# One-hot matrices of eight blocks by one comparison, and counting that waits for its own constants only

## The chip, the cores and the metric

The kernel runs on one core of one Trainium2 chip. The time is the device time of one execution in microseconds (us); of several runs the median is given. The core has five engines with instruction streams of their own that meet only through semaphores: TensorE (PE, with its weight loads as PEld), VectorE (DVE), ScalarE (ACT), GpSimd (POOL) and SyncE (SP), which here issues transfers. TensorE's granted clock is shown as a share of full speed (1.00 is 2.4 GHz, 0.50 is 1.2 GHz).

## The reference, cut to what matters

Two layers, each an attention and a mixture of experts, with a residual and a layer norm after each of the four. There are 2 x 2048 tokens of 128 numbers, so 4,096 tokens, 32 blocks of 128.

```python
x = layernorm(x + deltanet(x))
# experts, layer 0: one of 8 for each token
p = softmax(x @ gate_w); e = argmax(p); w = p[e]
x = layernorm(x + w * (gelu(x @ w1[e] + b1[e]) @ w2[e] + b2[e]))
x = layernorm(x + linear_attention(x))
# experts, layer 1: the best two of 8, weighted by a softmax over the two
logits = x @ Wr + br; (l, e) = top_k(logits, 2); c = softmax(l)
x = layernorm(x + sum(c[i] * (silu(x @ W1[e[i]]) * (x @ W3[e[i]])) @ W2[e[i]] for i in (0, 1)))
```

## The kernel before

The kernel sorts the tokens by expert before it multiplies. In the middle stage (`single_experts`, followed by `linear_attention` in the same block) a group is one of 8 experts, and the sorted tokens fill up to 39 tiles of 128 rows. In the pair stage (`stage_pairs`) a group is one of 28 pairs of experts, padded to half tiles, and there are up to 46 tiles. Before a stage can multiply it needs the sorted order. This is the routing, and it is the same in both stages:

- SP stores all tokens to a scratch tensor in memory, `xe_dram` (L1044 in the middle, L1852 in the pair stage), in one transfer. In the middle, ten other transfers stand ahead of it in SP's queue: the biases and what `linear_attention` will need.
- VectorE picks each token's group and writes `sel`, a 0/1 matrix in fp16 (L1219, L2096).
- TensorE counts (L1109, L1931): one small matmul for each group, which gives the tokens of each group in each block.
- VectorE multiplies the counts by a triangle (`upto`, L1225, L2101), TensorE adds them up over the blocks, and VectorE works out for every token its slot in the sorted order, and from it `col`, the tile, and `pos`, the row in the tile.
- The order has to be inverted: for each tile and row, which token stands there. For each of the 32 blocks VectorE makes a one-hot matrix `at_pos` (128 tokens x 128 rows; L1241, L2118) and a matrix `at_col` (128 tokens x 39 or 46 tiles) that holds the token's number, `code`, at its tile (L1242, L2119). TensorE multiplies the two and sums over the blocks (L1118, L1944). It waits before each block's matmul for the semaphore `hot`, which each `at_col` raises.
- VectorE reads the result into `read_at` (L1244; in the pair stage L2124 and L2125) and raises `decoded`. GpSimd waits for `decoded` and for `stored`, the landing of `xe_dram`, and then gathers the tiles' rows, one tile after another (L1094, L1909).
- VectorE works out which expert or pair each tile belongs to. TensorE packs these numbers into words with the matrix `pack` (L1122, L1948), VectorE copies them (L1249, L2137) and raises `read`. SP waits for `stored` and then `read` before it issues the weights of the tiles (L1051, L1861).

GpSimd fills the constants at the start of each stage. The semaphore `const` counts them. In the middle, 1 stands for the plain fills, 2 for the triangles `before` and `tri`, and 10 for the eight steps that fill `pack` (L1088). In the pair stage, 3 stands for everything but `pack`, and 7 for `pack` too. TensorE waits for the last of them ahead of counting (10 or 7); so does VectorE (10 ahead of `upto` in the middle, 7 ahead of `sel` in the pair stage).

In the middle, TensorE's stream has another piece of work between placing and the one-hot matmuls: `ready(pe)`, the preparation of the attention's weights (L1471, L1475, L1477, L1480), which waits for GpSimd and ScalarE.

The helper `link` raises a semaphore with an instruction and makes VectorE wait for it, because the next one reads its result. `spread(ap, n)` repeats each element of a row n times, innermost; `every(ap, n)` repeats the whole row n times.

Of the kernel before, what the change touches and what calls it, by code (L numbers as in the profile page):

```python
# [9 lines left out]
ALU = mybir.AluOpType  # L10
# [3 lines left out]
P = 128  # L14
B, L, D = 2, 2048, 128
BLOCKS = B * L // P
# [15 lines left out]
def spread(ap, n):  # L32

    return ap.unsqueeze(len(ap.shape)).broadcast_to([*ap.shape, n])
# [913 lines left out]
F16 = mybir.dt.float16  # L948
# [3 lines left out]
GR = (B * L + PAIRS * (HALF - 1)) // P + 1  # L952
ROUND = float(3 * 2 ** 22)
# [15 lines left out]
TILES = (B * L + E * (P - 1)) // P  # L969


def single_experts(nc, io, sb, tag, st, banks, w_in, wa, wb, b2):
# [3 lines left out]
    PACK = 8  # L976
# [20 lines left out]
    slot, col, pos = (tmp(n, [P, BLOCKS]) for n in ("slot", "col", "pos"))  # L997
    col_no, pos_no, code = tmp("col_no", [P, TILES]), tmp("pos_no", [P, P], F16), tmp("code", [P, BLOCKS])
    at_pos, at_col = tmp("at_pos", [P, BLOCKS, P], F16), tmp("at_col", [P, BLOCKS, TILES], F16)
# [18 lines left out]
    b1_in, b1_ps, b1_done, y_done, ranked = (sem(n) for n in ("b1_in", "b1_ps", "b1_done", "y_done", "ranked"))  # L1018
# [84 lines left out]
    def tensor(pe, ready):  # L1103
        pe.wait_ge(b1_in, 16)
        nc.tensor.transpose(psY[0][:, 0:E * NF], b1_rows[:, :], ident[0:E * NF, 0:E * NF]).then_inc(b1_ps, 1)
        pe.wait_ge(const, 2 + PACK)
# [9 lines left out]
        for n in range(BLOCKS):  # L1116
            pe.wait_ge(hot, n + 1)
            mm = nc.tensor.matmul(ps_found, at_pos[:, n], at_col[:, n], start=(n == 0), stop=(n == BLOCKS - 1))  # L1118
        mm.then_inc(found, 1)
        pe.wait_ge(numbered, 1)  # L1120
        pe.wait_ge(decoded, 1)
# [80 lines left out]
    def vector(dve):  # L1202
        v = nc.vector
        links = 0

        def link(ins):

            nonlocal links
            links += 1
            ins.then_inc(step, 1)  # L1210
            dve.wait_ge(step, links)
# [11 lines left out]
        dve.wait_ge(const, 2 + PACK)  # L1223
# [14 lines left out]
        link(v.tensor_scalar(col[:, :], col[:, :], ROUND, -ROUND, ALU.add, ALU.add))  # L1238
        link(v.scalar_tensor_tensor(pos[:, :], col[:, :], -float(P), slot[:, :], ALU.mult, ALU.add))
        for n in range(BLOCKS):  # L1240
            v.tensor_scalar(at_pos[:, n], pos_no[:, :], pos[:, n:n + 1], None, ALU.is_equal)  # L1241
            v.tensor_scalar(at_col[:, n], col_no[:, :], col[:, n:n + 1], code[:, n:n + 1], ALU.is_equal, ALU.mult).then_inc(hot, 1)  # L1242
# [524 lines left out]
def stage_pairs(nc, io, sb, tag, v_in, wac, wb):  # L1767
# [7 lines left out]
    with ExitStack() as st:  # L1775
        def tmp(name, shp, dt=F32):
            return st.enter_context(nc.sbuf_tensor(f"{tag}_{name}", shp, dt))

        def sem(name):
            return take(nc, f"{tag}_{name}")  # L1780

        def bank(name, shp):
# [17 lines left out]
        slot, col, pos = (tmp(n, [P, BLOCKS]) for n in ("slot", "col", "pos"))  # L1800
        col_no, pos_no, code = tmp("col_no", [P, GR]), tmp("pos_no", [P, P], F16), tmp("code", [P, BLOCKS])
        at_pos, at_col = tmp("at_pos", [P, BLOCKS, P], F16), tmp("at_col", [P, BLOCKS, GR], F16)
# [21 lines left out]
        ranked = sem("ranked")  # L1824
# [7 lines left out]
        def every(ap, n):  # L1832

            return ap.unsqueeze(1).broadcast_to([ap.shape[0], n, ap.shape[1]])
# [12 lines left out]
        with nc.Block(no_gpsimd_drain=True) as block:  # L1847
# [79 lines left out]
            def _(pe):  # L1927
                pe.wait_ge(const, 7)
# [13 lines left out]
                for n in range(BLOCKS):  # L1942
                    pe.wait_ge(hot, n + 1)
                    mm = nc.tensor.matmul(ps_found, at_pos[:, n], at_col[:, n], start=(n == 0), stop=(n == BLOCKS - 1))  # L1944
                mm.then_inc(found, 1)
                pe.wait_ge(paired, 1)
                pe.wait_ge(decoded, 2)
# [115 lines left out]
            def _(dve):  # L2063
                v = nc.vector
                links = 0

                def link(ins):

                    nonlocal links
                    links += 1  # L2070
                    ins.then_inc(step, 1)
                    dve.wait_ge(step, links)
# [22 lines left out]
                dve.wait_ge(const, 7)  # L2095
# [19 lines left out]
                link(v.tensor_scalar(col[:, :], col[:, :], ROUND, -ROUND, ALU.add, ALU.add))  # L2115
                link(v.scalar_tensor_tensor(pos[:, :], col[:, :], -float(P), slot[:, :], ALU.mult, ALU.add))
                for n in range(BLOCKS):
                    v.tensor_scalar(at_pos[:, n], pos_no[:, :], pos[:, n:n + 1], None, ALU.is_equal)  # L2118
                    v.tensor_scalar(at_col[:, n], col_no[:, :], col[:, n:n + 1], code[:, n:n + 1], ALU.is_equal, ALU.mult).then_inc(hot, 1)  # L2119
# [128 lines left out]
```

## Time and profile before

| | us |
|---|---|
| median of 3 runs | 779.83 |
| the three runs | 779.83, 772.30, 779.96 |
| profiled execution | 777.14 |
| its span in the trace | 775.4 |
| middle stage: first constant to first gather | 285.6 to 307.7 |
| pair stage: first constant to first gather | 551.0 to 583.1 |

Within the span TensorE is busy 618.8 us (80%), its weight loads 466.9 us (60%), VectorE 425.0 us (55%), ScalarE 351.9 us (45%) and GpSimd 286.6 us (37%). These shares are means over stages that have different limits. In the two routings the first tile's matmuls have not begun, and each engine waits for the one before it, so there the order of the steps counts and not the share. A row of the timeline gives the start, the length, the engine, the line and the operation, what it writes and reads with shapes, and in brackets how long the engine sat idle before and what released it. The tensors of both stages have the prefix `e_`, those of the attention `a_`; the memory banks of the middle stage are all called `mid_ps`.

### The profile page before, as it was taken

The page shows a single profiled execution, that of the slowest core. Times are in us where ns is not written, and L with a number is a line of the kernel's source. Part 1 is how long each engine was busy: PE and PEld are TensorE (multiplying, and loading weights), DVE is VectorE, ACT ScalarE, POOL GpSimd, SP SyncE. Part 2 cuts the span into 40 slices and gives each one's busy share as a digit, 9 for nine tenths or more (in the row PEclk, how much of TensorE's full clock was granted, in tenths as well). Part 3 has the DMA queues.
Part 4 walks back from the last instruction along what each step waited for, and adds up shares of the span by engine and source line. Part 5 has one row for each costly group of instructions (what it writes and reads, how often), then busy time and mean ns, then how long its engine had stood idle before and what let it go on. Part 6 is the DMA issues. An engine that isn't in the chain of part 4 may idle for free. (4 is left out here: it accounts for less than half of the span.)

```text
span 775.4 us, 40316 instructions
## 1 busy us (share of the span) xinstructions
PE 618.8 (80%) x16699; PEld 466.9 (60%) x16699; DVE 425.0 (55%) x1490; ACT 351.9 (45%) x935; POOL 286.6 (37%) x489
## 2 busy tenths in 40 slices
PE   4787545999998935899939899998147999999993
PEld 3665445988888923899926667666122455554552
DVE  4996370133332568155543546657594667767765
ACT  4764110222222660578843454644104555665562
POOL 2244302122211453444325336353404255455434
PEclk9997555799999685799976999999556999999997
DMA  4011112222222916566521111100063333333430
GB/s 122 2 39 39 38 54 71 71 91 92 92 85 76 339 53 123 173 194 210 171 62 46 36 28 37 30 27 8 1 110 82 94 102 110 100 100 106 104 96 12
DMA packets 70850, 66.45 MB, mean 86 GB/s; under 512 B 17183, under 2 KB 60366, under 8 KB 70512
## 3 DMA queue, kind: packets, MB, share of 16 engines
q1 hardware_dynamic: 65488, 55.43, 23.5%
q0 software_dynamic: 5280, 10.00, 6.1%
q8 instruction: 42, 0.69, 0.4%
q14 instruction: 40, 0.33, 0.2%
HBM read 20.70 MB, written 11.93 MB: 42 GB/s over the span
## 5 line engine op out<-in xcount | busy, mean ns | idle before, releaser
L1962 PE MATMUL e_psH<-wac,e_xT 128*64 x184 | 91.4, 620 | 0.8 <-ACT e_xT L2022 0.6
L1964 PE MATMUL e_psH<-e_up_w,e_xT 128*64 128x512 f32 x184 | 91.4, 621 | 0.0
L1909 POOL DMA_INDIRECT e_row<-xe_dram,e_read_at x46 | 44.6, 970 | 73.7 <-DVE spare L2150 45.3
L1914 POOL DMA_INDIRECT out<-spare,e_write_at x46 | 46.3, 1007 | 47.3 <-ACT spare L2039 36.9
L596 POOL TENSOR_TENSOR tb<-tinv,mb 128x128 f32<-128x128 f32 x64 | 24.3, 401 | 85.4 <-PE d_psY L610 85.4
L1094 POOL DMA_INDIRECT e_row<-xe_dram,e_read_at x39 | 37.0, 948 | 49.4 <-DVE spare L1258 34.6
L2143 DVE TENSOR_TENSOR e_h<-e_pre,e_psH 128x512 f32<-128x512 f32 x46 | 31.6, 687 | 42.9 <-ACT e_pre L2028 42.9
L2028 ACT ACTIVATE e_pre<-e_psH 128x512 f32<-128x512 f32 x46 | 27.5, 598 | 58.4 <-PE e_psH L1964 57.9
L1983 PE MATMUL e_psY<-vb,e_hT 128*64 x368 | 50.8, 282 | 2.9 <-issue 2.9
L1180 ACT ACTIVATE e_hT<-mid_ps,e_b 128x128 f32<-128x128 f32 x156 | 45.0, 381 | 15.1 <-PE mid_ps L1136 14.9
L1986 PE MATMUL e_psY<-e_down_w,e_hT 128*64 128x128 f32 x368 | 50.8, 282 | 0.0
L721 DVE TENSOR_TENSOR S<-d_psS,on 128x64 f32<-128x64 f32 x64 | 14.3, 223 | 60.7 <-PE d_psS L667 60.7
L1983 PEld LDWEIGHTS e_psY<-vb,e_hT 128*64 128x64 f32 x368 | 39.6, 138 | 10.7 <-issue 10.7
L1136 PE MATMUL mid_ps<-e_xT,e_up_w 128*128 128x128 f32 x312 | 44.4, 289 | 0.2 <-DMA e_up_w<-wa 0.2
L2016 ACT ACTIVATE e_up_w<-wac 128x512 f32 x46 | 28.8, 626 | 33.4 <-DVE e_words L2137 26.9
L1962 PEld LDWEIGHTS e_psH<-wac,e_xT 128*64 128x64 f32 x184 | 22.0, 139 | 34.4 <-issue 29.9
L1144 PE MATMUL mid_ps<-wb,e_hT 128*128 x312 | 42.2, 280 | 0.5 <-issue 0.4
L1973 PEld LDWEIGHTS e_psT<-ident,e_h 128*128 128x128 f32 x184 | 19.3, 140 | 36.7 <-issue 36.5
L1662 DVE TENSOR_TENSOR a_sc<-mid_ps,a_tri 128x512 f32<-128x512 f32 x64 | 40.9, 680 | 0.0
L1136 PEld LDWEIGHTS mid_ps<-e_xT,e_up_w 128*128 128x128 f32 x312 | 40.4, 202 | 0.6 <-issue 0.4
L1986 PEld LDWEIGHTS e_psY<-e_down_w,e_hT 128*64 128x64 f32 x368 | 39.6, 138 | 0.0
L1144 PEld LDWEIGHTS mid_ps<-wb,e_hT 128*128 128x128 f32 x312 | 38.7, 196 | 1.2 <-issue 1.0
(386 smaller groups left out, 1778.7 us busy)
## 6 DMA issues: line engine op xcount, KB each, us to landing
e_down_w<-vb SPq DMA_DIRECT2D x92, 128.0 KB, 2.0
e_up_w<-wa SPq DMA_DIRECT2D x39, 256.0 KB
xe_dram<-xe SPq DMA_DIRECT2D x2, 2080.0 KB, 13.2
vk_now<-vk SPq DMA_DIRECT2D x18, 192.0 KB, 2.1
kq_now<-kq SPq DMA_DIRECT2D x18, 192.0 KB, 2.1
gk_now<-gk SPq DMA_DIRECT2D x18, 128.0 KB, 2.0
outs_dram<-spare SPq DMA_DIRECT2D x9, 256.0 KB, 2.8
r<-in_L_attn_hidden_states SPq DMA_DIRECT2D x8, 256.0 KB, 4.6
```

The lines of the kernel that those rows point to most:

```text
L1094: pool.indirect_dma_start(out=row[g % ROWS][:, :], out_offset=None, in_=x_dram, in_offset=bass.IndirectOffsetOnAxis(ap=read_at[:, g:g + 1] ...
L1136: mm = nc.tensor.matmul(psH[g % 2][:, f], up_w[g % DEEP][:, f * P:(f + 1) * P], xT[g % 2][:, :], start=True, stop=True)
L1144: mm = nc.tensor.matmul(psY[g % 2][:, 0:D], hT[g % DEEP][:, f], wb[:, bass.ds(who * NF + f, 1)].rearrange("p a d -> p (a d)"), start=(f == ...
L1180: act.activation(hT[g % DEEP][:, f], psH[g % 2][:, f], ACT.Gelu, bias=b1[:, bass.ds(who * NF + f, 1)]).then_inc(h_done, 1)
L1662: ins = v.tensor_tensor(sc[:, g].rearrange("p k h l -> p (k h) l"), psS[g][:, :].rearrange("p (a l) -> p a l", l=HALF_T), tri[:, :].unsque ...
L1909: pool.indirect_dma_start(out=row[g % ROWS][:, :], out_offset=None, in_=x_dram, in_offset=bass.IndirectOffsetOnAxis(ap=read_at[:, g:g + 1] ...
L1914: pool.indirect_dma_start(out=out, out_offset=bass.IndirectOffsetOnAxis(ap=write_at[:, g:g + 1], axis=0), in_=z[:, g], in_offset=None, bou ...
L1962: nc.tensor.matmul(psH[g % 2][0:HALF, j], xT[g % 2][:, 0:HALF], wac[:, bass.ds(who[0][j], 1)].rearrange("p a f -> p (a f)"), start=True, s ...
L1964: mm = nc.tensor.matmul(psH[g % 2][HALF:P, j], xT[g % 2][:, HALF:P], up_w[g % 2][j][:, :], start=True, stop=True)
L1983: nc.tensor.matmul(psY[0:HALF, j], hT[g % 2][:, j, k * P:k * P + HALF], wb[:, bass.ds(who[0][j] * NF + k, 1)].rearrange("p a d -> p (a d)" ...
L1986: mm = nc.tensor.matmul(psY[HALF:P, j], hT[g % 2][:, j, k * P + HALF:(k + 1) * P], down_w[g % DEEP][:, j, k], start=(k == 0), stop=(k == N ...
L2143: v.tensor_tensor(h[g % 2][:, :, :], pre[g % 2][:, :, :], psH[g % 2][:, :, F:2 * F], ALU.mult).then_inc(h_done, 1)
```

## The change

For eight blocks at a time (`AHEAD = 8`), one `tensor_tensor` compares the numbers of the columns with `at`, one compares the numbers of the rows with `pos`, and one multiplies the first result by `code`. That is three instructions for eight blocks instead of two for each block. The small operands (`col_no`, `code`, and the new `at` and `pos`) become fp16, as `pos_no` and the results already are. `hot` is raised once in eight blocks, and TensorE waits for it before every eighth matmul. A new semaphore, `matched`, keeps the multiplication behind the comparison that it reads. The waits for `const` ahead of counting ask only for the constants that counting uses (2 and 3); the wait for `pack` stands before the matmul that reads it. The core of the diff, for the middle stage; the pair stage has the same with `GR` for `TILES`, 7 for `2 + PACK` and 3 for 2:

```diff
-    slot, col, pos = (tmp(n, [P, BLOCKS]) for n in ("slot", "col", "pos"))
-    col_no, pos_no, code = tmp("col_no", [P, TILES]), tmp("pos_no", [P, P], F16), tmp("code", [P, BLOCKS])
+    slot, col = tmp("slot", [P, BLOCKS]), tmp("col", [P, BLOCKS])
+    at, pos = tmp("at", [P, BLOCKS], F16), tmp("pos", [P, BLOCKS], F16)
+    col_no, pos_no, code = tmp("col_no", [P, TILES], F16), tmp("pos_no", [P, P], F16), tmp("code", [P, BLOCKS], F16)
...
-        pe.wait_ge(const, 2 + PACK)
+        pe.wait_ge(const, 2)
         pe.wait_ge(selected, 1)
...
         for n in range(BLOCKS):
-            pe.wait_ge(hot, n + 1)
+            if n % AHEAD == 0:
+                pe.wait_ge(hot, n // AHEAD + 1)
             mm = nc.tensor.matmul(ps_found, at_pos[:, n], at_col[:, n], start=(n == 0), stop=(n == BLOCKS - 1))
         mm.then_inc(found, 1)
         pe.wait_ge(numbered, 1)
+        pe.wait_ge(const, 2 + PACK)
...
-        dve.wait_ge(const, 2 + PACK)
+        dve.wait_ge(const, 2)
         dve.wait_ge(counted, 1)
...
-        link(v.tensor_scalar(col[:, :], col[:, :], ROUND, -ROUND, ALU.add, ALU.add))
-        link(v.scalar_tensor_tensor(pos[:, :], col[:, :], -float(P), slot[:, :], ALU.mult, ALU.add))
-        for n in range(BLOCKS):
-            v.tensor_scalar(at_pos[:, n], pos_no[:, :], pos[:, n:n + 1], None, ALU.is_equal)
-            v.tensor_scalar(at_col[:, n], col_no[:, :], col[:, n:n + 1], code[:, n:n + 1], ALU.is_equal, ALU.mult).then_inc(hot, 1)
+        link(v.tensor_scalar(at[:, :], col[:, :], ROUND, -ROUND, ALU.add, ALU.add))
+        link(v.scalar_tensor_tensor(pos[:, :], at[:, :], -float(P), slot[:, :], ALU.mult, ALU.add))
+        for c in range(BLOCKS // AHEAD):
+            s = slice(c * AHEAD, (c + 1) * AHEAD)
+            v.tensor_tensor(at_col[:, s], every(col_no[:, :], AHEAD), spread(at[:, s], TILES), ALU.is_equal).then_inc(matched, 1)
+            v.tensor_tensor(at_pos[:, s], every(pos_no[:, :], AHEAD), spread(pos[:, s], P), ALU.is_equal)
+            dve.wait_ge(matched, c + 1)
+            v.tensor_tensor(at_col[:, s], at_col[:, s], spread(code[:, s], TILES), ALU.mult).then_inc(hot, 1)
```

## Rows read from the trace of the kernel before

**Rows 1.** The page's part 4: the chain that ended last, by line.
```profile
PE e_psH L1962 11%; PE e_psY L1983 6%; PE e_psT L1973 3%; PE e_psX L1954 2%; DVE e_at_col L2119 1%; DVE e_at_pos L2118 1%; PE e_psY L1986 0%; DMA e_row<-xe_dram,e_read_at 0%; DMA e_br<-in_L_ffn_br 0%; POOL out L1914 0%; PE e_psX L1931 0%; PE e_psH L1964 0%; DVE e_picked L2110 0%; DVE e_upto L2101 0%; DVE e_sel L2096 0%
```

**Rows 2.** Timeline of the middle routing, 287 to 292: start, length, engine, line.
```profile
287.64 2.76 POOL L1088 TENSOR_SCALAR_AFFINE_SELECT e_pack<-e_pack 128x5 bf16<-128x5 bf16 x8
...
287.91 0.43 DVE L1219 TENSOR_TENSOR e_sel<-e_rank,e_key 128x256 f16<-128x256 f32 x1
...
288.70 0.35 DVE L1222 RECIPROCAL xe<-e_den 128x32 f32<-128x32 f32 x1
...
290.46 0.64 PE L1109 MATMUL mid_ps<-e_ones,e_sel 128*32 128x1 f16 x8 [3.01 <-POOL e_pack L1088]
...
290.74 0.38 SPq L1044 DMA_DIRECT2D xe_dram<-xe  x1
...
291.22 0.42 DVE L1225 TENSOR_TENSOR e_upto<-mid_ps,e_tri 32x264 f16<-32x264 f32 x1 [2.16 <-PE mid_ps L1109]
```

**Rows 3.** Timeline of the middle, from the one-hot loop to the first tile.
```profile
294.89 0.26 DVE L1241 TENSOR_SCALAR e_at_pos<-e_pos_no,e_pos 128x128 f16<-128x128 f16 x1
...
295.88 0.57 PE L1480 MATMUL mid_ps<-a_w,a_bo_mat 128*128 128x9 f32 x2 [0.36 <-ACT a_wY L1646]
...
296.30 0.45 PE L1118 MATMUL mid_ps<-e_at_col,e_at_pos 128*128 128x39 f16 x4
...
306.58 0.31 DVE L1242 TENSOR_SCALAR e_at_col<-e_col_no,e_col,e_code 128x39 f16<-128x39 f32 x1
...
306.94 0.22 PE L1118 MATMUL mid_ps<-e_at_col,e_at_pos 128*128 128x39 f16 x1 [0.15 <-DVE e_at_col L1242]
...
307.70 1.20 POOL L1094 DMA_INDIRECT e_row<-xe_dram,e_read_at  x1 [12.38 <-DVE e_read_at L1244]
...
308.18 0.15 DVE L1249 CAST e_words<-mid_ps 1x5 int32<-1x5 f32 x1 [0.26 <-PE mid_ps L1122]
...
309.47 15.45 SPq L1051 DMA_DIRECT2D e_up_w<-wa  x9
...
312.62 2.04 PE L1136 MATMUL mid_ps<-e_xT,e_up_w 128*128 128x128 f32 x8 [0.18 <-DMA e_up_w<-wa]
```

**Rows 4.** Transfers: the two writes, KB, us to landing; middle, then pair stage.
```profile
xe_dram<-xe SPq DMA_DIRECT2D x1, 2080.0 KB, 13.9
...
xe_dram<-xe SPq DMA_DIRECT2D x1, 2080.0 KB, 12.6
```

**Rows 5.** Timeline of the pair stage's routing, 553 to 584.
```profile
553.89 1.53 POOL L1893 TENSOR_SCALAR_AFFINE_SELECT e_pack<-e_pack 128x23 bf16<-128x23 bf16 x4 [0.16 <-POOL e_tri_no L1890]
...
559.89 1.09 DVE L2096 TENSOR_TENSOR e_sel<-e_pair_no,e_pair 128x896 f16<-128x896 f32 x1
...
560.90 0.25 DVE L2098 TENSOR_SCALAR e_den<-e_ex 128x32 f32<-128x32 f32 x1
...
562.13 0.36 SPq L1852 DMA_DIRECT2D xe_dram<-xe  x1
...
569.47 0.26 DVE L2118 TENSOR_SCALAR e_at_pos<-e_pos_no,e_pos 128x128 f16<-128x128 f16 x1
...
581.68 0.22 PE L1944 MATMUL e_psR<-e_at_col,e_at_pos 128*128 128x46 f16 x1 [0.15 <-DVE e_at_col L2119]
...
582.63 0.20 DVE L2125 TENSOR_TENSOR e_write_at<-e_token,e_empty 128x46 uint32<-128x46 f32 x1
...
583.12 1.07 POOL L1909 DMA_INDIRECT e_row<-xe_dram,e_read_at  x1 [21.02 <-DVE e_write_at L2125]
```

**Rows 6.** VectorE groups by form: busy us, mean ns of one, idle before.
```profile
L2118 DVE TENSOR_SCALAR e_at_pos<-e_pos_no,e_pos 128x128 f16<-128x128 f16 x32 | 8.1, 253 | 0.0
...
L2126 DVE TENSOR_SCALAR e_past<-e_ends,e_tile_no 128x28 f32<-128x28 f32 x1 | 0.2, 234 | 0.0
```

**Rows 7.** Windows: length, busy us (count) of PE, PEld, DVE, ACT, POOL, clock, DMA, GB/s.
```profile
312.00:321.00 9.00, 7.81 (x34) 7.28 (x35) 0.00 (x0) 5.03 (x16) 4.44 (x5) 0.50 0.60 193
321.00:324.00 3.00, 3.00 (x29) 3.00 (x28) 1.11 (x5) 1.76 (x7) 0.47 (x1) 0.99 0.32 122
588.00:594.00 6.00, 5.78 (x13) 1.50 (x15) 0.99 (x2) 2.61 (x4) 3.85 (x5) 0.50 0.74 202
```

More of the change, by code:

```diff
@@ L969 @@
 TILES = (B * L + E * (P - 1)) // P
+AHEAD = 8
 def single_experts(nc, io, sb, tag, st, banks, w_in, wa, wb, b2):
@@ L1017, in single_experts @@
         "read", "stored"))
-    b1_in, b1_ps, b1_done, y_done, ranked = (sem(n) for n in ("b1_in", "b1_ps", "b1_done", "y_done", "ranked"))
+    b1_in, b1_ps, b1_done, y_done, ranked, matched = (sem(n) for n in ("b1_in", "b1_ps", "b1_done", "y_done", "ranked", "matched"))
     row_in = [sem(f"row_in{i}") for i in range(ROWS)]
@@ L1799, in stage_pairs @@
         halves, ends, first, one = (tmp(n, [P, PAIRS]) for n in ("halves", "ends", "first", "one"))
-        slot, col, pos = (tmp(n, [P, BLOCKS]) for n in ("slot", "col", "pos"))
-        col_no, pos_no, code = tmp("col_no", [P, GR]), tmp("pos_no", [P, P], F16), tmp("code", [P, BLOCKS])
+        slot, col = tmp("slot", [P, BLOCKS]), tmp("col", [P, BLOCKS])
+        at, pos = tmp("at", [P, BLOCKS], F16), tmp("pos", [P, BLOCKS], F16)
+        col_no, pos_no, code = tmp("col_no", [P, GR], F16), tmp("pos_no", [P, P], F16), tmp("code", [P, BLOCKS], F16)
         at_pos, at_col = tmp("at_pos", [P, BLOCKS, P], F16), tmp("at_col", [P, BLOCKS, GR], F16)
@@ L1823, in stage_pairs @@
             "hot", "found", "decoded", "paired", "packed", "read", "stored", "bias_in"))
-        ranked = sem("ranked")
+        ranked, matched = sem("ranked"), sem("matched")
         row_in = [sem(f"row_in{i}") for i in range(ROWS)]
@@ L1927, in _ @@
             def _(pe):
-                pe.wait_ge(const, 7)
+                pe.wait_ge(const, 3)
                 pe.wait_ge(selected, 1)
@@ L1942, in _ @@
                 for n in range(BLOCKS):
-                    pe.wait_ge(hot, n + 1)
+                    if n % AHEAD == 0:
+                        pe.wait_ge(hot, n // AHEAD + 1)
                     mm = nc.tensor.matmul(ps_found, at_pos[:, n], at_col[:, n], start=(n == 0), stop=(n == BLOCKS - 1))
@@ L1946, in _ @@
                 pe.wait_ge(paired, 1)
+                pe.wait_ge(const, 7)
                 pe.wait_ge(decoded, 2)
@@ L2094, in _ @@
                 link(v.scalar_tensor_tensor(pair[:, :], hi[:, :], 0.5, lo[:, :], ALU.mult, ALU.subtract))
-                dve.wait_ge(const, 7)
+                dve.wait_ge(const, 3)
                 v.tensor_tensor(sel[:, :, :], every(pair_no[:, :], BLOCKS), spread(pair[:, :], PAIRS), ALU.is_equal).then_inc(selected, 1)
@@ L2114, in _ @@
                 link(v.tensor_scalar(col[:, :], slot[:, :], 1.0 / P, -127 / 256, ALU.mult, ALU.add))
[L2115 to L2119, printed above, removed]
+                link(v.tensor_scalar(at[:, :], col[:, :], ROUND, -ROUND, ALU.add, ALU.add))
+                link(v.scalar_tensor_tensor(pos[:, :], at[:, :], -float(P), slot[:, :], ALU.mult, ALU.add))
+                for c in range(BLOCKS // AHEAD):
+                    s = slice(c * AHEAD, (c + 1) * AHEAD)
+                    v.tensor_tensor(at_col[:, s], every(col_no[:, :], AHEAD), spread(at[:, s], GR), ALU.is_equal).then_inc(matched, 1)
+                    v.tensor_tensor(at_pos[:, s], every(pos_no[:, :], AHEAD), spread(pos[:, s], P), ALU.is_equal)
+                    dve.wait_ge(matched, c + 1)
+                    v.tensor_tensor(at_col[:, s], at_col[:, s], spread(code[:, s], GR), ALU.mult).then_inc(hot, 1)
                 dve.wait_ge(found, 1)
```

## Prediction

> **What bounds the kernel now.** I read the page first, then the chain of waits, then the timelines of the two routings, then single rows for durations. The chain that ended last [rows 1] shows the reader two things. The tail of the kernel is TensorE work of the pair stage (L1962, L1983, L1973), and in front of it stands the routing of that stage, with the two operations of the one-hot loop, `e_at_col` L2119 and `e_at_pos` L2118, as the largest VectorE entries. So what the routing of the pair stage saves arrives at the end one for one: nothing of the stage can start before the first gather. The chain ends at the start of that stage, so for the middle stage the waits have to be read in the program and the timeline.
>
> In the middle stage the order is: selection, counting, placing, 32 pairs of comparisons, decode, gather. Counting does not start when `e_sel` is ready (288.34) but when GpSimd's last fill of `e_pack` is (287.64 + 2.76 = 290.40), and TensorE starts at 290.46 [rows 2]. The one-hot loop then runs on VectorE from 294.89 to 306.89, its last matmul starts at 306.94, and the first gather at 307.70 [rows 3]. But the gather has a second condition, `stored`: the 2,080 KB write of `xe_dram` was issued at 290.74 [rows 2] and landed 13.9 us after its issue [rows 4], at 304.64. At present it is 3.06 us early. That is the cover I must not forget.
>
> In the pair stage `e_pack` was filled at 553.89 + 1.53 = 555.42, and `e_sel`, which comes before counting, only began at 559.89. The loop runs from 569.47, the last matmul starts at 581.68, the first gather at 583.12 [rows 5]. The write of `xe_dram`, issued at 562.13 [rows 5], landed after 12.6 us [rows 4], at 574.73, 8.4 us ahead of the gather.
>
> **The waits on constants.** In the pair stage all the waits for 7 were met 4.5 us before they were reached [rows 5], so 7 to 3 gives nothing. In the middle, counting may start at 288.34 plus the hand-over from `e_sel` to TensorE; the second constant is filled before `e_pack` (from 287.64) and is there. Where the last `at_col` released its matmul (306.89 to 306.94) the hand-over took 0.05 us [rows 3]; I take 0.1. That is 288.44 instead of 290.46, so 2.0 us. `e_upto` stood 0.76 us behind the start of counting (290.46 to 291.22) [rows 2]; it moves with it to 289.2. Its engine is free by then: the reciprocal ahead of it ended at 289.05 [rows 2]. The wait for all of `const` now stands before the matmul for the packed words, where it has long been met (290.40). What TensorE has queued between placing and the one-hot matmuls is the preparation for the attention stage; its last piece, L1480 at 295.88, hangs on GpSimd and ScalarE, not on counting, and does not move [rows 3]. It has a cost only if the first eight blocks are ready before it: they come at about 294.8, so the first group waits until 296.4, which the later groups absorb.
>
> **The one-hot loop.** Per block it issued one comparison for `at_pos` and one compare-and-multiply for `at_col`. 32 pairs took 12.0 us in the middle (294.89 to 306.89), 0.375 us a pair [rows 3]. It now issues three `tensor_tensor` per eight blocks: 8x39 or 8x46 elements, 8x128, and 8x39 or 8x46 again. The duration is the unknown. From the two rows of `e_sel`, 256 elements take 0.43 us and 896 take 1.09 us [rows 2, 5]: 0.66 us for 640 elements is 1.03 ns an element, and I take 1.04. From start to start, `e_sel` with 896 elements held the engine for 1.01 us (559.89 to 560.90) [rows 5], so an instruction costs 75 ns beyond its elements (0.935). Both are with a 32-bit source; the change has 16-bit sources only.
>
> Pair stage: 8x46 is 368 elements, 0.46 us; 1,024 elements, 1.14 us; 0.46 us again. That is 2.06 us a group, 8.25 us for four, plus 0.07 us for the drain of the last instruction and 0.06 us to TensorE. The wait on `matched` costs nothing, since the long `at_pos` comparison lies between the two instructions on `at_col`. The price of groups is at the end: before, one matmul was left after the last comparison; now eight are. Where four stood ready together, they took 0.45 us [rows 3], of which one is about 0.22 us, so a further matmul costs 0.08 to 0.11 us; seven at 0.10 are 0.7 us. The last matmul starts 8.25 + 0.13 + 0.7 = 9.08 us after the loop's start, where it was 12.21 us (569.47 to 581.68) [rows 5]. **Gain 3.1 us.** TensorE needs 0.8 us for a group and VectorE 2.06 us, so TensorE does not become the bound. The write, landed at 574.73, stays ahead of a gather at about 580.0.
>
> Middle: 312 elements cost 0.40 us, so 1.95 us a group and 7.8 us for four. First start to last matmul is 7.8 + 0.13 + 0.7 = 8.6 us against 12.05 (294.89 to 306.94) [rows 3], 3.4 us less. With the 2.0 us of the waits, the gather's addresses would be ready for 307.70 - 5.4 = 302.3. There the write is in the way: 304.64 at the earliest, 304.9 with the 0.29 us from the end of `e_write_at` (582.83) to the first gather as it stands in the pair stage [rows 5]. **Gain 2.8 us, not 5.4**; 2.6 us are lost on the write. The write itself is not moved: the ten transfers ahead of it in SP's queue hold it, not the routing. The expert weights of the first tile follow `stored` too: SP issued them at 309.47, 1.1 us after the words were stored (308.33) [rows 3]; the words now come before the landing, so it is 304.7 plus 1.1, 305.8, and they stay just ahead of the second transpose. So L1136, at 312.62 before, comes at 309.8.
>
> `pos` and `at` as 16-bit outputs have 32 elements each; their nearest rows are equally short and I put no cost on them, between 0 and 0.05 us. The bound of the element rate is open on both sides. Below: a one-source operation with 16-bit data, 128 elements, takes 253 ns, where one with 28 32-bit elements and the same pointer takes 234 ns [rows 6], 0.2 ns an element; so narrow data can be faster on this engine. Above: no row shows two 16-bit sources of which one repeats an element. I take 1.04 ns, the rate of the nearest row, `e_sel`, which has two sources with both kinds of repetition.
>
> The Trainium skill, page "Vector Engine (DVE) Microarchitecture Reference", section "Performance modes", lets a two-source operation produce two results a cycle when all operands are 16-bit and the innermost step of each is one; it reports that one element read 16 times as a source of such an operation ran at one result a cycle. Here one source of each of the three instructions repeats its element innermost, so by this page the narrow types buy no rate and the sum stays at 5.9 us; were the mode taken it would be 9.6 us, rival (a). No row here shows either.
>
> **The sum.** 2.8 + 3.1 = 5.9 us. The profiled execution took 777.14 us (775.4 us of span and 1.74 us around it), so 771.2 us. The median of the three runs shown is 779.83, which gives 773.9; the runs reach from 772.3 to 779.96, and the profiled one is between. I name 773.0.
>
> **Rivals.** (a) *Two elements a cycle.* Half the elements: 1.14 us a group in the pair stage, 5.4 us in all, gain 6.8; the write (574.73) is then still ahead of the gather (576.3). The middle stays at 2.8. Together 9.6 us: 767.5 for the profiled execution. For it: the one-source 16-bit row; against it: the repeated element. (b) *The write does not bind.* Then the middle gives 5.4 and the sum is 8.5: 768.6. For it: the same write took 1.3 us less in the pair stage [rows 4], so its length is not fixed; against it: nothing in the change makes it 2.3 us shorter. (c) *TensorE's clock takes it back.* After both routings TensorE works at half its clock (0.50, that is 1.2 GHz) until 321 and 594 [rows 7], some 8 us after its work begins in the middle (312.62) [rows 3] and 6 us in the pair stage. If these rises stay at their time instead of following the work, half of each stage's gain is lost: 1.4 and 1.55 us, sum 2.9, 774.2. (d) *Slower.* If the repeated 16-bit reads run below one element a cycle, the pair stage breaks even at (12.21 - 0.83 - 0.9) / 7.04 = 1.49 ns an element. In the middle the loop may take 14.05 us, and the limit is (14.05 - 1.73) / 6.59 = 1.87 ns. Both together turn at 1.67 ns. At two cycles an element (2.09 ns) the pair stage loses 4.2 and the middle 1.5 us: 782.8, slower than before. Against it: `e_sel` repeats too and holds 1.04.
>
> **How the numbers follow.** Forecast 0.72, (a) 0.08, (b) 0.04, (c) 0.12, (d) 0.04. About 1% (7.8 us) is what a measurement of this kernel can tell from no change. (a) and (b) are faster by over 1%; the forecast's 5.9 us lies below the bound, but the runs scatter by 7.7 us, and I give a fifth of it to the far side: faster 0.26. Slower by over 1% needs 2.2 ns an element or a disturbed comparison: 0.03. The rest, 0.71, is within 1%. The range: below, the fastest run less the sum, 772.3 - 5.9 = 766.4, which holds (a) and (b) for the profiled execution; above, 779, near the median less nothing, which holds (c) on the median (776.9) and leaves out (d).
>
> **What would show it.** In the profile after: `e_upto` of the middle about 2 us earlier; 1,024-element comparisons of 1.2 us (0.6 would be (a), 2.2 would be (d)); loops of 7.8 and 8.25 us; last matmul 0.7 us behind the last multiplication; the first gather of the middle right behind the landing at 304.6 with `e_read_at` over 2 us earlier ((b) if it comes at 302.3); the first gather of the pair stage 5.9 us earlier than 583.12. The prediction is wrong if the clock rises late in both stages, or if the write's landing moves.

## The result, and the profile after

| | before | after |
|---|---|---|
| median of 20 runs each, us | 779.68 | 771.33 |
| lowest run, us | 772.30 | 766.28 |
| profiled execution, us | 777.14 | 769.71 |
| its span, us | 775.4 | 768.0 |
| granted TensorE clock, mean | 0.854 | 0.871 |

The ratio of the runs is 0.9934, with a 95% interval from 0.9912 to 0.9957: about 5.1 us less (0.0066 x 779.68). The forecast was 773.0 and within 1%. The medians stand further apart (8.35 us, a quotient of 0.9893, which lies outside that interval), and the profiled executions 7.4 us. I go by the ratio, because it has an interval and because ten further runs of the changed kernel (e5 below) came out at 0.9938 again, there with medians 5.9 us apart. One run of each kernel was far off the others: 999.18 us before, and 806.44 us after, at a granted clock of 0.758.

First the timeline of the middle stage of the changed kernel (start and length in us, engine, line, operation, and in brackets the engine's idle time ahead and what ended it):

```profile
283.75 0.35 SPq L1042 DMA_DIRECT2D e_b_rows<-in_L_ffn_b  x1
...
287.42 0.42 DVE L1229 TENSOR_TENSOR e_upto<-mid_ps,e_tri 32x264 f16<-32x264 f32 x1 [0.15 <-PE mid_ps L1111]
...
288.94 0.38 SPq L1046 DMA_DIRECT2D xe_dram<-xe  x1
...
291.04 0.48 DVE L1246 TENSOR_TENSOR e_at_col<-e_col_no,e_at 128x312 f16<-128x312 f16 x1
291.11 1.79 POOL L1410 TENSOR_SCALAR a_tri_b<-a_tri_b,a_low 128x64 f32<-128x64 f32 x1
...
295.85 0.60 PE L1487 MATMUL mid_ps<-a_w,a_bo_mat 128*128 128x9 f32 x2 [0.85 <-POOL a_bo_mat L1418]
...
299.25 0.45 PE L1121 MATMUL mid_ps<-e_at_col,e_at_pos 128*128 128x39 f16 x8 [1.47 <-DVE e_at_col L1249]
299.73 0.20 DVE L1251 TENSOR_SCALAR e_read_at<-mid_ps 128x39 uint32<-128x39 f32 x1 [0.54 <-PE mid_ps L1121]
...
304.00 1.20 POOL L1096 DMA_INDIRECT e_row<-xe_dram,e_read_at  x1 [6.64 <-DMA xe_dram<-xe]
```

SP's transfer in the first row waits for nothing of the routing, so I measure every kernel's middle stage from it: it is at 283.75 here, 285.54 before. From there `e_upto` comes at 3.67 us (before 5.68), the last group of one-hot matmuls at 15.50 (before the last matmul at 21.40), `e_read_at` at 15.98, and the first gather at 20.25 (before 22.16). The last row names the new bound: GpSimd sat idle until the *write* of `xe_dram`, where before it sat idle until `e_read_at` [rows 3]. The addresses were ready at 299.93 and lay for four microseconds.

The same for the pair stage:

```profile
548.82 0.35 SPq L1858 DMA_DIRECT2D e_br<-in_L_ffn_br  x1
...
567.26 0.54 DVE L2129 TENSOR_TENSOR e_at_col<-e_col_no,e_at 128x368 f16<-128x368 f16 x1
567.72 1.22 DVE L2130 TENSOR_TENSOR e_at_pos<-e_pos_no,e_pos 128x1024 f16<-128x1024 f16 x1
568.86 0.53 DVE L2132 TENSOR_TENSOR e_at_col<-e_at_col,e_code 128x368 f16<-128x368 f16 x1
569.31 0.53 DVE L2129 TENSOR_TENSOR e_at_col<-e_col_no,e_at 128x368 f16<-128x368 f16 x1
...
575.57 0.49 PE L1953 MATMUL e_psR<-e_at_col,e_at_pos 128*128 128x46 f16 x8 [1.55 <-DVE e_at_col L2132]
...
577.27 1.06 POOL L1917 DMA_INDIRECT e_row<-xe_dram,e_read_at  x1 [17.39 <-DVE e_write_at L2138]
```

A group takes 2.05 us (567.26 to 569.31). From SP's first transfer of the stage the loop starts at 18.44 us (before 18.48), and the first gather comes at 28.45 (before 32.13). Here it is `e_write_at` that ends the wait, as before [rows 5]; the write has long landed.

### The profile page after: what moved, and what is told of

It reads as the page before. It is cut to its first block and busy times, and to the rows that moved or that the text cites. A ratio compares the mean times of both kernels' runs of the same rounds, so it can differ in the third digit from the quotient of the medians.

```text
span 768.0 us, 40212 instructions
## 1 busy us (share of the span) xinstructions
PE 601.2 (78%) x16699; PEld 457.2 (60%) x16699; DVE 416.7 (54%) x1386; ACT 351.7 (46%) x935; POOL 290.3 (38%) x489
## 5 line engine op out<-in xcount | busy, mean ns | idle before, releaser
L1184 ACT ACTIVATE e_hT<-mid_ps,e_b 128x128 f32<-128x128 f32 x156 | 45.0, 381 | 14.0 <-PE mid_ps L1140 13.9
```

The lines of the kernel that those rows point to most:

```text
L1184: act.activation(hT[g % DEEP][:, f], psH[g % 2][:, f], ACT.Gelu, bias=b1[:, bass.ds(who * NF + f, 1)]).then_inc(h_done, 1)
```

## Experiments

The experiments ran in three groups, each beside its own runs of the kernel before: the first four kernels (before: 776.09 us), the next three (775.36), and the last two on another chip, on which the kernel before itself took 821.41 us; times are compared inside a group, by their ratio. Distances are counted as above, from SP's first transfer of the stage, and this table holds them (us). The column on the pair stage's matmuls gives the start of the last group of eight, or of the last single one in the two kernels with the old loops:

| kernel | middle: `e_read_at` | write issued | it took | first gather | first up matmul | pair stage: last matmuls | first gather | ratio to before (95%) |
|---|---|---|---|---|---|---|---|---|
| before | 21.66 | 5.20 | 13.9 | 22.16 | 27.08 | 30.69 | 32.13 | 1 |
| after | 15.98 | 5.19 | 14.2 | 20.25 | 25.35 | 26.75 | 28.45 | 0.9934 (0.9912 to 0.9957) |
| e1_waits_only | 19.85 | 5.20 | 14.1 | 20.36 | 25.35 | 30.65 | 32.08 | 0.9942 (0.9910 to 0.9974) |
| e2_onehot_only | 17.69 | 5.20 | 14.7 | 20.79 | 25.91 | 26.75 | 28.45 | 0.9973 (0.9932 to 1.0014) |
| e3_wide_operands | 15.99 | 5.20 | 13.5 | 19.63 | 24.82 | 26.79 | 28.50 | 0.9918 (0.9889 to 0.9948) |
| e4_pairs_packed | 15.99 | 5.19 | 14.1 | 20.19 | 25.26 | 23.08 | 25.21 | 0.9857 (0.9794 to 0.9920) |
| e5_changed_again | 15.99 | 5.20 | 14.5 | 20.56 | 25.63 | 26.74 | 28.45 | 0.9938 (0.9899 to 0.9977) |
| e6_early_write | 21.92 | 3.21 | 16.6 | 22.43 | 27.36 | 26.75 | 28.45 | 0.9961 (0.9915 to 1.0007) |
| e7_packed_early | 20.98 | 3.21 | 15.5 | 21.49 | 26.43 | 23.11 | 25.25 | 0.9914 (0.9879 to 0.9950) |
| e8_packed_again | 15.99 | 5.20 | 13.8 | 19.93 | 25.07 | 23.09 | 25.23 | 0.9867 (0.9833 to 0.9902) |
| e9_late_loads | 17.28 | 3.20 | 13.9 | 18.01 | 23.54 | 23.81 | 25.94 | 0.9866 (0.9831 to 0.9902) |

**One half of the change at a time.** The first kernel has the new waits on constants and the old loops; the second the new loops and the old waits:

```
e1:  - pe.wait_ge(const, 2 + PACK)     + pe.wait_ge(const, 2)      # and as changed elsewhere
     the loops of 32 blocks as before
e2:  - pe.wait_ge(const, 2)            + pe.wait_ge(const, 2 + PACK)
     the loops of four groups as changed
```

> The kernel before with the waits for constants of the change and its old one-hot loop. Times are counted from SP's first transfer of the stage (285.54 before, 283.75 in the changed kernel). Theory W (the landing of the write of xe_dram bounds the middle once the routing is faster): counting starts 2.0 us earlier, the addresses are ready at about 19.9 instead of 21.9, just behind the landing (5.2 + 13.9 to 14.2 = 19.1 to 19.4), and the first gather moves from 22.2 to 20.2, nearly where the changed kernel has it (20.25). The pair stage keeps its 32.1 us from the first transfer to the first gather. In all 2.0 us less, 0.26%. Rival A (the two edits add up in the middle): the gather moves by the 2.0 us here as well, but then the loop alone must show as much again. Rival N: the wait for the packing constants was covered by something else, and the gather stays at 22.2.

> The changed kernel with the old waits for constants. Theory W: counting starts 2.0 us later than in the changed kernel, the loop takes as long, the addresses are ready at about 18.0 to 18.4, still ahead of the write's landing at 19.1 to 19.4, so the first gather of the middle stays at 20.25 and the kernel costs the same as the changed one: the waits are worth nothing beside the loop. Rival A: the first gather comes 2.0 us later than in the changed kernel, at 22.2 less the gain of the loop. In the pair stage the last one-hot matmul stands 8.6 us behind the loop's start in both theories, against 12.2 before.

The waits alone bring the middle's gather to 20.36, 1.80 us earlier; with the one-hot groups added it is 20.25. So in the middle stage the two halves don't add up (1.80 and 1.37 us alone, 1.91 together): each alone brings the routing to the write, and the later gather of e2 (20.79) goes with a write that took 0.5 us longer. In the pair stage it is the other way round: the waits give nothing (32.08 against 32.13) and the groups everything (28.45, as in the whole change). The middle of e1, near the gather:

```profile
301.53 0.20 DVE L1245 TENSOR_SCALAR e_read_at<-mid_ps 128x39 uint32<-128x39 f32 x1 [0.31 <-PE mid_ps L1118]
302.04 1.20 POOL L1094 DMA_INDIRECT e_row<-xe_dram,e_read_at  x1 [10.58 <-DVE e_read_at L1245]
```

and of e2:

```profile
299.63 0.20 DVE L1250 TENSOR_SCALAR e_read_at<-mid_ps 128x39 uint32<-128x39 f32 x1 [0.54 <-PE mid_ps L1121]
302.73 1.20 POOL L1096 DMA_INDIRECT e_row<-xe_dram,e_read_at  x1 [9.71 <-DMA xe_dram<-xe]
```

In e1 the gather stands 0.31 us behind the end of the addresses; the write had landed at 300.98 (281.68 + 5.20 + 14.1), 1.06 us before it; with the 0.86 to 0.93 us that a gather needs behind a landing, it could have gone at most 0.2 us earlier. In e2 the addresses had been ready for 2.9 us, and the gather stands 0.89 us behind the landing (281.94 + 5.20 + 14.7 = 301.84). The times of the whole kernel can't tell the halves apart: their intervals overlap, and the gains at stake are 1.9 to 5.6 us, against runs that scatter by over 10. They even stand in the wrong order: by the gathers e1 gains 1.85 us and e2 5.05, by the ratios it is 0.58% (4.5 us) and 0.27% (2.1 us). Over all ten kernels the check is better. The gains of the two gathers, each from one profiled execution and taken as a share of the kernel before, run from 0.24% in e1 to 1.26% in e9. They lie inside the interval of the ratio for nine of the ten, and for e1 just below it (0.26% to 0.90%).

**The width of the operands.** Everything as in the changed kernel, but `at`, `pos`, `code` and the column numbers in 32 bits. The row numbers `pos_no` and the one-hot matrices stay at 16:

```
- at, pos = tmp("at", [P, BLOCKS], F16), tmp("pos", [P, BLOCKS], F16)
+ at, pos = tmp("at", [P, BLOCKS]), tmp("pos", [P, BLOCKS])
- col_no, ..., code = tmp("col_no", [P, GR], F16), ..., tmp("code", [P, BLOCKS], F16)
+ col_no, ..., code = tmp("col_no", [P, GR]), ..., tmp("code", [P, BLOCKS])
```

> The changed kernel with at, pos, code and the column numbers in 32 bits; the row numbers and the two results stay 16-bit. Theory R (one of the two sources repeats an element, and so the narrow types buy no rate): the comparison of 1,024 elements takes 1.22 us as in the changed kernel, the loop of the pair stage 8.6 us, the time is the same within 0.3%. Rival: the 16-bit sources do help, and the comparison takes clearly over 1.22 us here. Open beside it: in the changed kernel GpSimd's small operations next to the middle loop took up to 1.79 us where they took 0.45 before. If that comes from long two-source VectorE operations it stays; if from 16-bit sources it goes.

The 1,024-element comparison by tile, in e3 (count; min/median/max ns; first and last start; form), where one source is 32-bit:

```profile
L2130 DVE TENSOR_TENSOR e_at_pos<-e_pos_no,e_pos x4: 1215/1216/1218, 570.8 to 576.9; 128x1024 f16<-128x1024 f16 x4
```

and in the changed kernel, where both are 16-bit:

```profile
L1247 DVE TENSOR_TENSOR e_at_pos<-e_pos_no,e_pos x4: 1210/1260/1354, 291.4 to 297.6; 128x1024 f16<-128x1024 f16 x4
...
L2130 DVE TENSOR_TENSOR e_at_pos<-e_pos_no,e_pos x4: 1217/1218/1219, 567.7 to 573.8; 128x1024 f16<-128x1024 f16 x4
```

1,216 and 1,218 ns: the narrow types buy nothing here. (A row gives the type of one source only; that `pos` is 32-bit in e3 is in its code.) All that was won in the loop is the number of instructions.

**The same elements in another order.** Is it the repeated element? In the pair stage the number of the block was made the innermost index, so that the source with one value for each block is read with step one, and the source with the numbers is stored eight times over (the middle stage is left as it was):

```
+ col_no = tmp("col_no", [P, GR, AHEAD], F16); pos_no = tmp("pos_no", [P, P, AHEAD], F16)
+ at_pos = tmp("at_pos", [P, BLOCKS // AHEAD, P, AHEAD], F16)      # at_col likewise
- v.tensor_tensor(at_pos[:, s], every(pos_no[:, :], AHEAD), spread(pos[:, s], P), ALU.is_equal)
+ v.tensor_tensor(at_pos[:, c], pos_no[:, :, :], every(pos[:, s], P), ALU.is_equal)
- mm = nc.tensor.matmul(ps_found, at_pos[:, n], at_col[:, n], ...)
+ mm = nc.tensor.matmul(ps_found, at_pos[:, n // AHEAD, :, n % AHEAD], at_col[:, n // AHEAD, :, n % AHEAD], ...)
```

> The changed kernel; in the pair stage alone the eight blocks lie innermost in both matrices: the row and column numbers are filled eight times each, and at, pos and code are repeated as whole rows of eight, so that no source repeats an element innermost and all are 16-bit. Theory R, from the Trainium skill's page Vector Engine (DVE) Microarchitecture Reference, section Performance modes: two results a cycle, so 1,024 elements take 0.53 + 0.15 = 0.68 us instead of 1.22 and 368 take 0.34 instead of 0.53; a group takes 1.14 instead of 2.04 us, and the first gather of the pair stage comes 3.6 us earlier, 24.8 us after the stage's first transfer instead of 28.4. In all 3.6 us less than the changed kernel. Rival 1: the rate stays, and nothing changes. Rival 2: TensorE reads its operands with a step of eight elements, and its eight matmuls of a group, 0.49 us in the changed kernel, get longer than VectorE's 1.14 us; then they bound the loop.

By tile, in e4:

```profile
L1953 PEld LDWEIGHTS e_psR<-e_at_col,e_at_pos x32: 142/148/170, 566.3 to 570.2; 128*128 128x128 f16 x32
L1953 PE MATMUL e_psR<-e_at_col,e_at_pos x32: 262/272/289, 566.3 to 570.3; 128*128 128x46 f16 x32
...
L2130 DVE TENSOR_TENSOR e_at_pos<-e_pos_no,e_pos x4: 681/684/684, 565.3 to 568.7; 128x1024 f16<-128x1024 f16 x4
```

The same 1,024 comparisons now take 684 ns instead of 1,218: 0.52 ns an element beside a fixed part (both instructions on `at_col` went from 534 to 342 ns). A group takes 1.12 us instead of 2.05. TensorE pays some of it back, since its operands now lie 16 bytes apart: 148 ns instead of 117 for a load of weights, 272 instead of 211 for a matmul, and the last eight matmuls take 0.92 us instead of 0.49. The first gather comes at 25.21, 3.24 us earlier than in the changed kernel; 3.6 was expected, and the longer tail on TensorE is the difference. The ratio to before is 0.9857 from four runs, and from six runs on the other chip 0.9867. By the ratios these kernels lie about 0.7% under the changed one (0.9934), but the first of the two intervals reaches into that of the changed kernel, and the second comes from another chip; against the kernel before both intervals lie wholly below 1.

The changed kernel and the packed one were each run once more as a measure of the scatter:

> The changed kernel once more, beside the two that follow. Theory W: first gather of the middle 20.2 us after SP's first transfer of the stage, give or take what the write's landing varies (13.5 to 14.7 us so far), about 0.9 us behind the landing; first gather of the pair stage at 28.45; 0.7 to 0.9% less than before. It also tells how far the profiled times of one kernel lie apart.

> The pair stage with the eight blocks innermost, once more, to narrow the interval. First gather of the middle at about 20.2 us and of the pair stage at 25.2 us after SP's first transfer of the stage, as before. Changed kernel's gain (5.9 us by the ratio of e5_changed_again and the first result, 0.7%) plus 3.2 us: a ratio of 0.988 to 0.990. The 0.9857 of the first time came from few executions.

e5 repeats the changed kernel's middle but for the length of the write: 14.5 instead of 14.2, and the gather 0.31 later. Its profiled execution took 763.4 us, 6.3 less than that of the changed kernel with the same code. More than the whole effect of the change lies between two executions of one kernel.

**The write earlier.** If the write sets the middle's gather, an earlier write must bring it forward. With the load of the experts' biases, `e_b_rows`, eleven transfers and not ten stand ahead of it in SP's queue. First, ScalarE issues the ten of them that are for the attention stage, and `den` and its reciprocal go ahead of `sel` on VectorE; then the same with packed pairs:

```
- rows[0](sp, ready[0])          + rows[0](sp, lambda sp: None)
- rows[3](act, ready[3])         + rows[3](act, lambda act: (ready[0](act), ready[3](act)))
```

> The changed kernel; in the middle VectorE makes the weights (den, its reciprocal) ahead of sel, and the ten loads for the attention are issued by ScalarE after its copy of the biases, so that the write of xe_dram stands second in SP's queue. Theory W: the write is issued 2.5 us after SP's first transfer instead of 5.2, as soon as the reciprocal is there; the routing gets 0.7 us later (addresses at 16.9 instead of 16.2) and stays ahead. If the write takes its 14 us, the first gather comes at 17.5 instead of 20.2, 2.7 us less in all. Rival 1: the loads now run beside the write and lengthen it by what they move, some 0.3 MB beside 2.08 MB, 1 to 2 us, so that 1 to 1.7 us are left. Rival 2: the biases land behind the write, GpSimd waits for them, L1487 and with it the one-hot matmuls come late, and the gather stays at 20 or later. Rival A (the write does not bind): nothing, or 0.7 us more.

> The pair stage with the eight blocks innermost (first gather 3.2 us earlier than in the changed kernel, as in the run of it alone) and the early write of the middle. Theory W: the two stages add, so 3.2 plus what the early write gives alone (1 to 2.7 us) under the changed kernel, 4.2 to 5.9 us; against the kernel before 10 to 12 us, a ratio of 0.985 to 0.987. Rival: the early write costs as much as it gives, and the ratio is that of the packed pair stage alone.

In e6 the gather came later, at 22.43. Its timeline:

```profile
285.24 0.38 SPq L1046 DMA_DIRECT2D xe_dram<-xe  x1
...
301.90 0.29 POOL L1418 COPY a_bo_mat<-a_bo_col 128x128 f32<-128x128 f32 x1 [10.36 <-DMA a_b_o<-in_L_attn_wo_b]
...
302.69 1.23 PE L1121 MATMUL mid_ps<-e_at_col,e_at_pos 128*128 128x39 f16 x32
...
304.46 1.20 POOL L1096 DMA_INDIRECT e_row<-xe_dram,e_read_at  x1 [1.98 <-DVE e_read_at L1251]
```

The write left 2 us earlier, but beside the loads it took 16.6 us, and the small loads of biases came in behind it: GpSimd waited 10.36 us for one of them. TensorE's preparation for the attention stage hangs on it, and all 32 one-hot matmuls are queued behind that preparation. The first thing that the earlier write did was to delay a small load that stood in the way of everything. With packed pairs (e7) it was the same: the write took 15.5 us, the middle's gather came at 21.49, 1.3 us later than in e4, and the ratio is 0.9914 where 0.985 to 0.987 was expected.

So the last kernel (packed pairs, `den` first) puts the write second in SP's queue, the loads behind it, and moves what needs the loads behind the routing on the other engines:

```
   sp:    - ready(sp) ahead of the write          + ready(sp) behind it, ahead of the wait for `stored`
   pe:    - ready(pe) ahead of the one-hot matmuls + ready(pe) behind the matmul for the packed words
   pool:  - bo_mat, bqm ahead of the gathers       + behind the second gather
```

> The same pair stage; in the middle the weights are made ahead of sel, the write of xe_dram stands second in SP's queue, and the ten loads for the attention stand behind it. TensorE's and ScalarE's preparation for the attention follows the packed words, and GpSimd's part that needs the biases follows its second gather. Theory W: nothing runs beside the write now, so it takes about 12.5 us as in the pair stage, from 3.2 to 15.7; the addresses are ready at about 16.4 (the loop starts at 8.0, 0.7 later than in the changed kernel, and ends its matmuls 8.7 later), so the first gather comes at 16.8 to 17.1 instead of 20.2, 3.2 us less, and addresses and landing meet. Rival 1: the loads land so late (behind the write, at about 18) that the preparation delays the first tile's transposes, and the first up-projection, 25.3 before, gains 1 us or less. Rival 2: the write takes 14 us all the same: gather at 18.1.

```profile
285.63 0.38 SPq L1045 DMA_DIRECT2D xe_dram<-xe  x1
286.06 6.33 SPq L1380 DMA_DIRECT2D a_w_raw<-in_L_attn_wq_w  x1
...
299.71 0.20 DVE L1253 TENSOR_SCALAR e_read_at<-mid_ps 128x39 uint32<-128x39 f32 x1 [0.54 <-PE mid_ps L1122]
300.44 1.20 POOL L1096 DMA_INDIRECT e_row<-xe_dram,e_read_at  x1 [8.51 <-DVE e_read_at L1253]
```

Now the write is issued 3.20 us behind the first transfer instead of 5.19. It takes 13.9 us all the same, where 12.5 was expected with nothing beside it. It lands at 17.1, and the gather stands at 18.01, 2.24 us earlier than in the changed kernel and 1.92 earlier than in e8, with a slower `e_read_at` (17.28 instead of 15.98). That the gather moves forward while its addresses move back is the plainest sign that in the changed kernel the write held it. Here the two come so close together (landing 299.5, addresses 299.91) that the row names `e_read_at`; but the gather stands 0.53 us behind the addresses, where 0.31 was enough in e1, and 0.91 behind the landing, so it is still the write. The first up matmul follows 1.5 us earlier than in e8. Of this nothing is to be seen in the time: the ratios are 0.9866 and 0.9867. Part of it went in the pair stage, where e9 starts its loop 0.7 us later (19.17 against 18.45). There VectorE waits for the load of the router's biases, `e_br` (4 KB), which took 3.2 us to land in e9 and 2.5 us in every other kernel; why is open. The rest is inside the scatter. Both are about 1.3% under the kernel before, and they have the lowest ratios of this study, with e4, which is e8's kernel.

## Why the prediction was right, point by point

**The waits on constants: exact.** `e_upto` came 2.01 us earlier (5.68 to 3.67), where 2.0 was predicted; in the pair stage nothing, as predicted, which e1 shows alone.

**The loop: right in total, from two terms that were a little off.** Predicted were 1.14 us for 1,024 elements from start to start and 2.06 us a group; measured 1.14 (567.72 to 568.86) and 2.05. The rate of `e_sel`, 1.04 ns an element, held for two 16-bit sources ((1,218 - 534) ns for 1,024 - 368 elements). Break-even, rival (d), lay at 1.49. The tail was mis-sized: I took 0.7 us for the seven further matmuls, from four that took 0.45 together [rows 3]. All eight take 0.49 us in the pair stage, where one took 0.22 [rows 5]: 0.27 for seven, 0.04 each. Those four in [rows 3] were a bad row to read a slope from. That is 0.43 of the 0.58 us by which the pair stage's gain exceeded the forecast (3.68 us against 3.1); the rest are hundredths in the drain and in the start of the loop. From the end of the matmuls to `e_write_at` it is 0.73 us in both kernels (30.91 to 31.64, and 27.24 to 27.97).

**What was said not to move did.** The prediction held that TensorE's preparation for the attention stage does not move. Its last piece, L1487, came 12.10 us behind SP's first transfer instead of 10.34, because GpSimd worked more slowly beside the new comparisons (below). The first two groups of one-hot matmuls stood behind it (they start at 296.30), and the third group came 0.05 us behind its last multiplication again; so this step was wrong and cost nothing.

**The write in the middle: the mechanism right, its size 0.9 us too large.** `e_read_at` came 5.7 us earlier (21.66 to 15.98), and the gather only 1.91, because of the write. Predicted was 2.8. Two terms account for it. The write took 14.2 us instead of 13.9. And I had put the gather 0.29 us behind the landing, the distance from the end of `e_write_at` to the gather [rows 5]; that is a hand-over from VectorE to GpSimd, not from a transfer. Behind a landing the gather stands 0.86 us in the changed kernel (303.14 to 304.00), 0.89 in e2, 0.86 in e5 and 0.93 in e3. These are 0.3 and 0.57 us: 2.8 - 0.87 = 1.93. The prediction had named a landing that moves as a sign against it; it moved by these 0.3 us, inside what the same write differs by from kernel to kernel (13.5 to 14.7 us). Rival (b), that the write does not bind, is refuted by e2, and by e9, where the gather follows the write forward.

What follows the gather moved with it: the first up matmul came 1.73 us earlier (27.08 to 25.35).

**Rival (a), two elements a cycle, did not happen, and e4 shows why.** The Trainium skill, page "Vector Engine (DVE) Microarchitecture Reference", section "Performance modes", lets a two-source operation produce two results a cycle only if all operands are 16-bit with an innermost step of one. The trace agrees on the innermost step: 1,218 ns with the repeated element and 684 ns for the same elements without it, all 16-bit in both. That the rate in the packed order also needs the 16-bit types is not shown, since no run has packed 32-bit sources. I had given it the lower chance for the repeated element, and that is the reason that the runs bear out.

**Rival (c), the clock, did not happen.** Windows of the changed kernel (length; busy us and count of PE, PEld, DVE, ACT, POOL; granted clock; DMA share, GB/s):

```profile
313.00:314.00 1.00, 0.05 (x1) 0.08 (x1) 0.00 (x0) 1.00 (x6) 0.94 (x1) 0.94 0.50 134
...
586.00:587.00 1.00, 1.00 (x5) 0.39 (x7) 0.40 (x1) 0.82 (x2) 0.71 (x1) 0.91 0.82 266
```

The clock is up from 313.1 in the middle (0.94 in this window) and from 586.2 in the pair stage (0.91), where it was half until 321 and 594 [rows 7]. From the first up matmul that is 4.0 us (309.10) and 3.9 us (582.25), before 8.4 (312.62) and 5.9 (588.23). So it took nothing back. That it came even earlier than the work can't be put down to the change, at least not in the middle. There it rose 2.7 us behind the first up matmul in e5, the same kernel, and 8.0 us behind it in e3, whose routing takes the same time. The window of e5, then of e3:

```profile
309.00:310.00 1.00, 1.00 (x8) 0.93 (x7) 0.00 (x0) 1.00 (x1) 0.69 (x2) 0.76 0.21 54
```

```profile
315.00:316.00 1.00, 1.00 (x9) 1.00 (x8) 0.00 (x0) 0.99 (x4) 0.00 (x0) 0.72 0.09 27
```

What decides it was not tried. My estimate from these rows: 5.3 us more at half the clock are at most 2.7 us of TensorE work, so this can be a part of the scatter.

**The sum.** The two gathers gained 1.91 + 3.68 = 5.6 us, where 5.9 was predicted, and the runs say 5.1. That the total came so close is partly luck: the middle gave 0.9 us less than predicted, the pair stage 0.6 us more. And the interval of the runs (3.4 to 6.9 us) is too wide to check terms of this size; only the distances in the traces do. The 7.4 us between the two profiled executions hold more than that, in stretches that the change does not touch. SP's first transfer of the middle came 1.8 us earlier. From the first up matmul of the middle to SP's first transfer of the pair stage it took 238.4 us before and 239.7 after, but 234.9 in the repetition of the same kernel and up to 244.6 in e1 (e8 and e9, on the other chip, left out). From the first up matmul of the pair stage to the end it took 187.2 and 185.7. Part of this scatter can be seen in the attention stage, whose matmuls here and there stop for over 2 us for nothing that the profile shows; the view of the waits has this as "issue" (sum, times, longest). Before:

```profile
PE mid_ps L1557 <- issue: 2.2, 1, 2.2
```

In the changed kernel, where the same line is L1564:

```profile
PE mid_ps L1564 <- issue: 4.7, 2, 2.5
```

and in its repetition, e5:

```profile
PE mid_ps L1564 <- issue: 0.3, 1, 0.3
```

With e8 and e9 left out, the two kernels without such a stop there, e5 and e4, have the shortest way from the middle's first up matmul to the pair stage (234.9 and 235.8 us; the others 238.4 to 244.6). The cause of these stops stays open; it was not tried.

## What to carry to other kernels

Before speeding up the chain that computes addresses, look for the second condition of the gather, and count its margin: here 3 us of cover were all that the middle stage had to give, and two edits that would each have used it gave little more together than one. When many small comparisons are joined into one with broadcast sources, the gain is in the instructions, not in the types; if the width is to count as well, put the index that the broadcast repeats outermost and see what the strided operands cost on TensorE (here 0.93 us a group won on VectorE, 0.43 us on the last eight matmuls lost). And what stands ahead of a large transfer in a queue may be small loads that others need: moving the transfer ahead pays only when the consumers of those loads are moved behind.

## What the runs showed of the hardware that I had not expected

**Long two-source operations on VectorE hold GpSimd up.** In the changed kernel `a_tri_b` took 1.79 us (the timeline of the middle, above), while VectorE was in its group comparisons. The same instruction in e2, where it ran before the loop (count; min/median/max ns):

```profile
L1409 POOL TENSOR_SCALAR a_tri_b<-a_tri_b,a_low x1: 457/457/457, 289.3 to 289.3; 128x64 f32<-128x64 f32 x1
```

Two further ones in the changed kernel, the first with the comparison beside it:

```profile
293.50 1.35 DVE L1247 TENSOR_TENSOR e_at_pos<-e_pos_no,e_pos 128x1024 f16<-128x1024 f16 x1
...
293.74 1.18 POOL L1414 TENSOR_TENSOR a_heads<-a_heads 128x8 f32<-128x8 f32 x1
...
295.79 1.56 POOL L1420 TENSOR_SCALAR a_bqm<-a_mr,a_bq 128x4 f32<-128x4 f32 x1
```

Before they took 0.22 us, just ahead of the old loop, and 0.31 us, beside it. With `a_tri_b` (0.45 us before) each is longer by 0.96 to 1.34 us, up to about one comparison of 1,024 elements. VectorE loses less: the comparisons of the middle stage take 1,210 to 1,354 ns, those of the pair stage, where GpSimd is idle, 1,217 to 1,219. In e3, with 32-bit sources, `a_tri_b` takes 1,791 ns as well, so it is not a matter of the types. The Trainium skill, page "SBUF — State Buffer", section "Who interferes with whom", says that a VectorE instruction with two inputs in SBUF contends with a GpSimd instruction that reads SBUF, and calls the hold on the ports they share an exclusive lock. The lengths of GpSimd's operations agree, and the plainest is `a_heads`: it started at 293.74, 0.24 us into a comparison that ended at 294.85, and ended at 294.92. Which port they share no run here can show. It cost nothing here: what it delayed, the matmuls at L1487, held up two groups of one-hot matmuls, but not the last. In a kernel where that preparation is the bound, the joined comparisons would be paid for on GpSimd.

**It also goes the other way.** In the three kernels that make the reciprocal ahead of `sel` (e6, e7, e9), a VectorE instruction on 8 elements starts just behind GpSimd's long fill of `a_vm`, and ends with it. In e9:

```profile
287.60 1.00 POOL L1403 MEMSET a_vm<- 128x1088 f32 x1
287.65 0.97 DVE L1234 TENSOR_SCALAR e_count<-e_count 128x8 f32<-128x8 f32 x1
```

It took 0.97 to 0.98 us there and 0.17 in all other kernels, where it ran clear of that fill. With the later `sel` this is most of the 1.67 us by which the one-hot loop of e9's middle starts later than in the changed kernel (8.96 us against 7.29).

**The hand-over from a landed transfer to GpSimd's indirect DMA took 0.86 to 0.93 us**, that from a VectorE result 0.29 to 0.31. **The write of 2,080 KB took 13.5 to 14.7 us** in nine middle stages where SP alone issued the loads, ahead of it or, in e9, behind it, and 15.5 and 16.6 us where ScalarE's queue issued loads beside it. In e9 the first load behind the write held SP for 6.33 us (`a_w_raw` in e9's rows), where the same load ahead of it had taken 0.41 us before (285.94 to 286.35).
